# Normalised rows laid out by blocks of 32 columns, so that the transfers that move the blocks take one run per partition

## What is computed

```python
h = jnp.maximum(_layernorm(x, axis=-1), 0.0)
q = _split_heads(h @ Wq + bq); k = _split_heads(h @ Wk + bk); v = _split_heads(h @ Wv + bv)
scores = einsum('bhqd,bhkd->bhqk', q, k) / sqrt(HD) + beta * adj[:, None]
scores = where(adj[:, None] > 0, scores, -9e15)
probs = softmax(scores, axis=-1)
x = x + einsum('bhqk,bhkd->bhqd', probs, v)   # heads put side by side again
```

## Time and profile before

| what | value |
|---|---|
| median of 3 runs | 561.96 us (561.63 to 563.57) |
| the profiled execution, its own time | 562.12 us |
| its span, first to last instruction | 559.1 us |
| TensorE busy | 540.6 us, 97% of the span |
| ScalarE busy | 468.6 us, 84% |
| VectorE busy | 443.6 us, 79% |
| granted TensorE clock, mean | 0.995 of full speed |

### The profile page before, as it was taken

How to read it: one execution, slowest core, us unless ns; L and a number is a source line. 1 busy time by engine, 2 the same in 40 slices (tenths; PEclk the granted TensorE clock), 3 DMA queues, 4 the chain that set the end, 5 groups by cost and what they waited for, 6 DMA issues and landing times.

```text
span 559.1 us, 17693 instructions
## 1 busy us (share of the span) xinstructions
PE 540.6 (97%) x5568; PEld 458.4 (82%) x5568; DVE 443.6 (79%) x2265; ACT 468.6 (84%) x1867; POOL 127.8 (23%) x205
## 2 busy tenths in 40 slices
PE   8989999999999999999999999999999999999873
PEld 8778888888888888888888888888888888888662
DVE  5888888888888888888888888888888878756661
ACT  3558889988888988888898888889888888987885
POOL 4512221221222222122212212222221211011111
PEclk9999999999999999999999999999999999999997
DMA  8522242332424233242423334242423221000001
GB/s 245 160 76 43 63 103 57 100 80 61 109 61 102 55 89 84 63 108 59 107 55 87 82 67 109 56 109 54 107 67 68 53 69 31 31 30 28 18 30 42
DMA packets 115431, 42.22 MB, mean 76 GB/s; under 512 B 89136, under 2 KB 115376, under 8 KB 115376
## 3 DMA queue, kind: packets, MB, share of 16 engines
q1 hardware_dynamic: 115376, 41.59, 29.5%
HBM read 18.75 MB, written 12.58 MB: 56 GB/s over the span
## 4 chain that ended last, share of the span: by engine, by line
PE 88%; DVE 2%; issue 2%; ACT 1%; POOLq 0%; POOL 0%; DVEq 0%
PE G_ps L659 33%; PE S_ps L720 17%; PE PT_ps L704 16%; PE S_ps L679 10%; PE PT_ps L690 9%; PE PT_ps L710 3%; DVE probs L586 2%; ACT probsT L422 1%; DVE y L597 0%; ACT probs L414 0%; POOLq L73 0%; POOL y L385 0%; PE S_ps L730 0%; DVE negmax L586 0%; DVE h_lo L518 0%
## 5 line engine op out<-in xcount | busy, mean ns | idle before, releaser
L414 ACT ACTIVATE probs<-probs,negmax 128x128 f32<-128x128 f32 x768 | 298.9, 401 | 0.0
L586 DVE CUSTOM_DVE_ANT_0 probs<-S_ps,bias 128x128 f32<-128x128 f32 x768 | 164.4, 287 | 4.0 <-PE S_ps L679 4.0
L414 ACT ACTIVATION_READ_ACCUMULATOR probs<-probs,negmax 128x1 f32 x768 | 153.3, 200 | 0.0
L385 POOL TENSOR_TENSOR y<-y,x_ring 128x384 f32<-128x384 f32 x64 | 64.5, 1008 | 361.4 <-DVE y L597 361.4
L422 ACT COPY probsT<-PT_ps 128x512 f32<-128x512 f32 x192 | 106.3, 586 | 15.8 <-PE PT_ps L704 15.2
L659 PE MATMUL G_ps<-h_hi,w_hi 128*128 128x512 f32 x288 | 117.7, 409 | 0.0
L659 PE MATMUL G_ps<-h_hi,w_lo 128*128 128x512 f32 x288 | 117.5, 408 | 0.0
L659 PE MATMUL G_ps<-h_lo,w_hi 128*128 128x512 f32 x288 | 116.1, 403 | 0.0
L704 PE MATMUL PT_ps<-ident,probs 128*128 128x128 f32 x768 | 109.2, 277 | 5.0 <-DVE y L597 3.3
L704 PEld LDWEIGHTS PT_ps<-ident,probs 128*128 128x128 f32 x768 | 86.4, 141 | 15.9 <-issue 3.6
L567 DVE COPY outT<-PT_ps 128x384 f32<-128x384 f32 x64 | 35.7, 558 | 51.9 <-PE PT_ps L690 49.8
(11 more groups left out here) (42 smaller groups left out, 659.8 us busy)
## 6 DMA issues: line engine op xcount, KB each, us to landing
out_dram<-y SPq DMA_DIRECT2D x64, 192.0 KB, 1.9
x_ring<-in_x_dram SPq DMA_DIRECT2D x15, 768.0 KB, 5.3
xhat_moved<-xhat SPq DMA_DIRECT2D x416, 24.0 KB, 1.9
adj_in<-in_adj_dram SPq DMA_DIRECT2D x16, 256.0 KB, 3.0
x_ring<-in_x_dram SPq DMA_DIRECT2D x4, 192.0 KB, 3.2
w_raw<-in_L_gnn_Wk_dram SPq DMA_DIRECT2D x1, 576.0 KB, 7.6
w_raw<-in_L_gnn_Wv_dram SPq DMA_DIRECT2D x1, 576.0 KB, 8.6
w_raw<-in_L_gnn_Wq_dram SPq DMA_DIRECT2D x1, 384.0 KB, 4.6
```

The lines of the kernel that those rows point to most:

```text
L385: nc.gpsimd.tensor_tensor(y[:, z.s % 2, :], y[:, z.s % 2, :], x_ring[:, bass.ds(at, D)], ALU.add).then_inc(y_ready, 1)
L414: last = nc.scalar.activation(p, p, ACT.Exp, bias=negmax[:, e, j * KC + m:j * KC + m + 1], scale=TURN, accum_out=rowsum[:, e, m * HC + j:m ...
L586: last = nc.vector.tensor_tensor_reduce(probs[:, a, j, m, :], S_ps[:, j, m * N:(m + 1) * N], bias[(z.par + 1) % 2][:, z.s, :], 1.0, LARGES ...
```

## The change

The `xhat` of groups 3 to 15 goes to a tensor of its own, `xhat_blocks`, in another order of columns. For each pair of sequences the four block columns c stand outermost, then the two sequences s, then the three thirds k, then 32 columns. What a transfer moves, all (s, k) of one c, is then one run of 192 numbers (768 bytes) in a partition, where it was six runs of 32 (128 bytes). `xhat_moved` has the same order. VectorE writes and reads the new order through strided views. Groups 0 to 2 keep the old `xhat`.

```diff
+        RUN = 2 * KC * HD
+        xhat_blocks = sb("xhat_blocks", [P, 2 * HC * RUN])
-        xhat_moved = sb("xhat_moved", [P, GROUP, D])
+        xhat_moved = sb("xhat_moved", [P, 2 * HC * RUN])
...
+        def blocks_of(tile, s):
+            pair = tile[:, s // 2 * HC * RUN:(s // 2 + 1) * HC * RUN]
+            return pair.rearrange("p (c s k e) -> p s k c e", c=HC, s=2, k=KC)[:, s % 2, :, :, :]
...
-                        came = xhat[r * HD:(r + 1) * HD, s0:s0 + 2, :].rearrange("p s (k c e) -> p (s k) c e", c=HC, e=HD)[:, :, c, :]
-                        goes = xhat_moved[c * HD:(c + 1) * HD, s0:s0 + 2, :].rearrange("p s (k r e) -> p (s k) r e", r=HC, e=HD)[:, :, r, :]
+                        came = xhat_blocks[r * HD:(r + 1) * HD, at + c * RUN:at + (c + 1) * RUN]
+                        goes = xhat_moved[c * HD:(c + 1) * HD, at + r * RUN:at + (r + 1) * RUN]
...
-                nc.vector.tensor_scalar(xhat[:, s % GROUP, :], x_ring[:, bass.ds(at, D)], meanvar[:, s, 0:1],
+                if isinstance(q, int) and q < 3 * GROUP:
+                    goes, came = xhat[:, s % GROUP, :], x_ring[:, bass.ds(at, D)]
+                else:
+                    goes, came = blocks_of(xhat_blocks, s % GROUP), x_ring[:, bass.ds(at, D)].rearrange("p (k c e) -> p k c e", k=KC, c=HC)
+                nc.vector.tensor_scalar(goes, came, meanvar[:, s, 0:1],
                                         rstd[:, s:s + 1], ALU.subtract, ALU.mult).then_inc(xhat_ready, 1)
...
-                nc.vector.transpose(hT[:, z.s % 2, :], xhat_moved[:, z.s, :]).then_inc(hT_ready, 1)
+                nc.vector.transpose(hT[:, z.s % 2, :].rearrange("p (k r e) -> p k r e", k=KC, r=HC), blocks_of(xhat_moved, z.s)).then_inc(hT_ready, 1)
```

More of the change, by code:

```diff
@@ L307, in move_blocks @@
             def move_blocks(pair, rows):
-                s0 = 2 * pair
+                at = pair * HC * RUN
                 for r in rows:
                     for c in range(HC):
-                        came = xhat[r * HD:(r + 1) * HD, s0:s0 + 2, :].rearrange("p s (k c e) -> p (s k) c e", c=HC, e=HD)[:, :, c, :]
-                        goes = xhat_moved[c * HD:(c + 1) * HD, s0:s0 + 2, :].rearrange("p s (k r e) -> p (s k) r e", r=HC, e=HD)[:, :, r, :]
+                        came = xhat_blocks[r * HD:(r + 1) * HD, at + c * RUN:at + (c + 1) * RUN]
+                        goes = xhat_moved[c * HD:(c + 1) * HD, at + r * RUN:at + (r + 1) * RUN]
                         sp.dma_start(goes, came).then_inc(blocks_moved[pair], 16)
```

## The result

The changed kernel takes 567.17 us (median of 5 runs, 565.51 to 568.57) against 561.96 us for the kernel before (5 runs). The ratio is 1.0078, 95% interval [1.0059, 1.0096]: slower by 0.8%, or 4.4 us (the two medians by themselves are 5.2 us apart), where 571.6 us and 9.6 us more were forecast. The direction and the place were right, the size was twice too large. The profiled execution has a span of 563.7 us against 559.1.

What follows compares the result with a forecast made beforehand. TensorE, busy 540.6 of 559.1 us, was taken as the bound. 48 slots x 0.20 us for `xhat` gave 9.6 us, the other terms 0; 562.12 + 9.6 = 571.7, stated as 571.6 us, range 567 to 579.

Steps and rivals of the forecast that it cites:

- The place: VectorE from L690 to `y`: no slack, the weight load waiting for `y` starts 0.11 to 0.12 us after it.
- `xhat` loses its fast pace: VectorE's `xhat` at L507: two elements at a time become one, 0.20 us more, bounds 0.11 and 0.31.
- equal cuts: VectorE's `xhat`: the fast pace needs input and output cut at the same element; a half falls inside a third.
- The transfers are hidden, and their packets worth nothing: The 416 block transfers: 66,560 of 115,431 packets go, nothing waits for them, worth 0.
- The transpose: VectorE L513: reads twelve runs of 32, stays at 571 ns, worth 0; at most 0.2 us more.
- 48 slots: Steps 2 to 13, four slots each: the 0.20 us is lost anew in every one, 9.6 us in all.
- It takes 0.14 us and its matmul starts right behind it, so the matmul is late by the same 0.20.: TensorE's weight load that waits for `y`: its whole delay of 0.20 us passes to the matmul and everything behind.
- rival 1: VectorE's `xhat` keeps its fast pace, TensorE never waits, time 562.0 us; decides at 0.00 us; chance 0.14.
- groups that keep 32.7 us: Sign on TensorE: if `xhat_blocks` is long and groups keep this pace, the mechanism is wrong.
- a delay of TensorE equal to the growth of `xhat`: Sign in a slot: if TensorE's delay equals that growth, whatever it is, only the size is wrong.

Runs made afterwards that it cites:

- the seven shapes: The kernel before with 28 normalisations of 384 elements, four of each shape, added at the end of VectorE's program: 0.48, 0.55 or 0.67 us each.
- 96 columns: The kernel before with a VectorE memset of 96 columns between `xhat` and `rinv` in steps 2 to 13: 562.51 us, ratio 1.0001.
- 160 columns: The kernel before with a VectorE memset of 160 columns between `xhat` and `rinv` in steps 2 to 13: 563.77 us, ratio 1.0009.

## Why the prediction was right in kind and wrong in size

- *The place*: the stretch of VectorE from L690 to `y`, with the weight load that waits for `y` 0.11 to 0.12 us behind it. Right: a pure delay in this stretch gives the same loss, and the same long `xhat` outside it gives none.
- *`xhat` loses its fast pace.* Right, 0.44 to 0.63 us in the slots, 0.19 more against 0.20 forecast. The guess at a mechanism (equal cuts) was borne out by the seven shapes. The rule that the prediction cites from the Trainium skill ("VectorE: DVE Perf Modes", section "Mode 2×_2P — use both read ports for one tensor") holds in them too: the trace agrees, with 0.48 us for outermost counts of 384, 2 and 4, 0.55 for 3 on both sides, and 0.67 for 3 against 384.
- *The transfers are hidden, and their packets worth nothing.* Right, shown from both sides: long runs with a fast `xhat` (ratio 0.9999), short runs with a slow one (1.0091).
- *The transpose.* Right, 571 to 569 ns.
- *48 slots.* Right: 48 new waits of 0.196 us.
- *"It takes 0.14 us and its matmul starts right behind it, so the matmul is late by the same 0.20."* This step failed. The start of the weight load was late by 0.19, and the matmul by 0.06 to 0.07, the ones after it by 0.09. I had taken the 0.14 us of the load's record as time that must pass ahead of the matmul. It need not. The 0.17 us between load and matmul in the earlier trace rows are the pace of the matmuls ahead, whose turn this one waits for, and in the tail, where nothing else held it, the matmul started 0.03 us after the load (522.94 in the earlier trace rows). That row was in the profile before and I did not read on to it:

```profile
522.97 0.41 PE L704 MATMUL PT_ps<-ident,probs 128*128 128x128 f32 x2 [0.62 <-DVE y L597]
```

The first matmul alone would let its load come 0.156 - 0.031 = 0.125 us late. Why the spare time is only 0.10 us shows at the second matmul of the batch; these figures are medians over the 48 slots. It starts 0.107 to 0.110 us after its own load in every kernel. Its load starts when the first matmul does, as long as that leaves room: 0.158 us after the first load in the kernel before, 0.103 with 96 columns. But where the first load is late, the second follows it by 0.057 to 0.060 us, and it never came sooner than 0.055. The first load stands 0.156 us ahead of its matmul before, so it can be 0.156 - 0.057 = 0.10 us late before the second matmul is. With 160 columns this alone is seen, the second load and the second matmul being the fourth and the last row:

```profile
288.71 0.19 PEld L723 LDWEIGHTS S_ps<-w_hi,h_lo 128*128 128x128 f32 x1
288.88 0.34 PE L723 MATMUL S_ps<-w_hi,h_lo 128*128 128x384 f32 x1
...
289.02 0.14 PEld L707 LDWEIGHTS PT_ps<-ident,probs 128*128 128x128 f32 x1
289.09 0.14 PEld L707 LDWEIGHTS PT_ps<-ident,probs 128*128 128x128 f32 x1
...
289.06 0.30 PE L707 MATMUL PT_ps<-ident,probs 128*128 128x128 f32 x1
289.19 0.38 PE L707 MATMUL PT_ps<-ident,probs 128*128 128x128 f32 x2
```

The first matmul is on time, 0.18 us after the last one of the values, the second is 0.137 us behind it (median), where 0.108 is the pace, and that is the whole loss of 0.027 us in the slot. In the changed kernel the first is 0.066 us late and the second another 0.029, together the 0.09 of the table to within a few ns. What holds the second load 0.057 us behind the first, no run took apart.

So the spare time was not nil but 0.10 us, the sum is 48 x (0.19 - 0.10) = 4.3 us, 33.03 us a group in place of 33.5, and rival 1 decides at 0.10 us and not at 0.00. With 562.0 this gives 566.3, within the 565.5 to 568.6 of the runs. The prediction named two ways of being off, groups that keep 32.7 us or a delay of TensorE equal to the growth of `xhat`; it was neither, the delay was half of the growth. That the median of 567.17 lies just inside the range of 567 to 579 is luck: its lower end stands for an `xhat` that grows by 0.11 us and is paid in full, and `xhat` grew by 0.19.

## What to carry to other kernels

A wait that ends exactly when its signal arrives is not yet a wait that costs: look at the start of the next matmul, and find a place in the same trace where nothing else holds it, to learn how much of the time between is needed. Look at the ones behind it too, since the second may be late before the first is. To price a delay, put a small idle instruction of growing size in the place; three doses give the spare time and the slope. Before giving an operation a strided view, ask whether its input and output can still be cut in two at the same element, and if not, go through the same elements in another order.

## What the runs showed that was not expected

A weight load of 128 columns is recorded with 0.14 us, and its matmul can start 0.03 us after the load's start. The Trainium skill says so in "TensorE: Matmul & The Clock Gate", section "Architectural detail: the array is 16× 32×32, not 1× 128×128": a matmul can begin before its weight load is complete. The trace agrees, with 0.03 us, and by this rule the 0.14 us need not have been taken as time that must pass. Further, the length of `xhat` depends on its neighbours: 445 ns behind the transpose and 472 ns behind `v` in the kernel before, 633 and 665 ns in the changed one. Where these 0.03 us come from was not tried.
